# Attention probabilities scaled by the inverse mass on GpSimd ahead of the value products, with a new order on all engines

## What is computed

```python
x = x + attn_ref(layernorm(x), ...)              # RWKV: time mixing with a scan over tokens, then channel mixing
x = x + xattn_ref(layernorm(x), ctx, ctx)        # attention between the 16 heads of each token
x = x + ffn_ref(layernorm(x), U1, V1, b1, U2, V2, b2)   # low-rank feed-forward with gelu
```

```python
scores = einsum('bsqd,bskd->bsqk', qh, kh) / sqrt(16)     # 16 x 16 per token
scores = where(tril, scores, -1e18)
attn   = softmax(scores, axis=-1)
out    = einsum('bsqk,bskd->bsqd', attn, vh)
```

## Time and profile before

| | us |
|---|---|
| median of 3 runs | 1115.2 (1113.61 to 1116.03) |
| the profiled execution | 1110.05 |
| its span from first to last instruction | 1108.1 |

### The profile page before, as it was taken

One profiled execution on the slowest core, in us unless ns is written; L12 is line 12 of the kernel. 1 busy time (PEld: TensorE's weight loads), 2 busy tenths in 40 slices (PEclk: granted clock), 3 DMA queues, 4 the chain that ended last, 5 costly groups with the idle time before them and its releaser, 6 DMA issues.

```text
span 1108.1 us, 15665 instructions
## 1 busy us (share of the span) xinstructions
PE 977.9 (88%) x4160; PEld 613.5 (55%) x4160; DVE 956.1 (86%) x2185; ACT 863.3 (78%) x1585; POOL 903.4 (82%) x862
## 2 busy tenths in 40 slices
PE   4689698999999999999999999999999999889505
PEld 2347274756556474756556574757566574646303
DVE  5846899999999999999999999999999899777561
ACT  4876769799797979798897979798897969573603
POOL 0223989989898989989898989899898989898880
PEclk9799799999999999999999999999999999999756
DMA  7110020111110111111111011111111011111001
GB/s 235 38 38 1 0 58 1 20 58 20 58 19 18 41 20 57 19 57 20 57 19 33 25 19 57 19 57 20 57 21 38 1 20 39 20 39 20 20 0 39
DMA packets 38317, 38.72 MB, mean 35 GB/s; under 512 B 2660, under 2 KB 37864, under 8 KB 38248
## 3 DMA queue, kind: packets, MB, share of 16 engines
q1 hardware_dynamic: 29800, 29.58, 8.4%
q0 software_dynamic: 8448, 8.39, 5.2%
HBM read 29.58 MB, written 8.39 MB: 34 GB/s over the span
## 4 chain that ended last, share of the span: by engine, by line
ACT 25%; POOL 24%; DVE 21%; issue 17%; PE 8%; DVEq 0%; POOLq 0%; ACTq 0%
POOL prod L351 18%; DVE psum L1646 7%; ACT n L484 5%; ACT hidden L619 4%; PE psum L895 4%; POOL prod L329 3%; DVE stat L1420 3%; ACT v_dh L588 2%; ACT xr L509 2%; DVE psum L1587 2%; DVE x L1595 2%; ACT rr L546 1%; ACT xk L509 1%; ACT e L542 1%; PE psum L949 1%
## 5 line engine op out<-in xcount | busy, mean ns | idle before, releaser
L329 POOL TENSOR_TENSOR prod<-q,kv_ctx 128x256 f32<-128x256 f32 (+5 forms) x448 | 360.2, 859 | 65.9 <-ACT q L484 65.9
L351 POOL TENSOR_TENSOR prod<-prob,v_dh 128x256 f32<-128x256 f32 (+3 forms) x256 | 384.4, 1703 | 12.8 <-ACT prob L594 12.8
L895 PE MATMUL psum<-xk,w_key 128*128 128x512 f32 x512 | 230.7, 604 | 14.1 <-DVE xk L1483 14.1
L1646 DVE TENSOR_REDUCE psum<-prod 128x64 f32<-128x256 f32 (+3 forms) x256 | 192.2, 821 | 50.0 <-POOL prod L351 49.0
L949 PE MATMUL psum<-w_val,hidden 128*128 128x256 f32 x1024 | 226.3, 379 | 0.0
L949 PEld LDWEIGHTS psum<-w_val,hidden 128*128 128x128 f32 x1024 | 193.5, 190 | 32.5 <-issue 7.7
L1617 DVE TENSOR_REDUCE score<-prod 128x16 f32<-128x256 f32 (+5 forms) x448 | 176.0, 475 | 11.6 <-POOL prod L329 11.6
L895 PEld LDWEIGHTS psum<-xk,w_key 128*128 128x128 f32 x512 | 97.6, 193 | 131.4 <-issue 120.7
L444 ACT ACT_TABLE_LOAD x96 | 123.2, 1283 | 2.6 <-PEq L1805 0.9
L909 PE MATMUL psum<-ident,n 128*128 128x128 f32 x384 | 59.5, 288 | 68.2 <-ACT n L484 52.8
L909 PEld LDWEIGHTS psum<-ident,n 128*128 128x128 f32 x384 | 46.9, 148 | 98.2 <-issue 68.9
(11 more groups left out here) (97 smaller groups left out, 1782.9 us busy)
## 6 DMA issues: line engine op xcount, KB each, us to landing
x_in<-in_x SPq DMA_DIRECT2D x16, 512.0 KB, 5.3
kv_ctx<-in_ctx SPq DMA_DIRECT2D x16, 512.0 KB, 4.5
x<-in_x POOLq DMA_DIRECT2D x16, 512.0 KB, 5.8
out<-x SPq DMA_DIRECT2D x16, 512.0 KB, 3.3
w_key<-in_wkey SPq DMA_DIRECT2D x1, 1024.0 KB
w_val<-in_wval SPq DMA_DIRECT2D x1, 1024.0 KB
w_v<-in_v SPq DMA_DIRECT2D x2, 256.0 KB
w_k<-in_wk SPq DMA_DIRECT2D x1, 256.0 KB, 4.8
```

Of the source, the lines that this page charges most:

```text
L329: ins = pool.tensor_tensor(o, a, b, ALU.mult)
L351: ins = pool.tensor_tensor(o, ph[:, HB * n:HB * n + HB, 0:keys].unsqueeze(2).to_broadcast(shape), vh[:, :, 0:keys].unsqueeze(1).to_broadca ...
L895: mm = pe.matmul(to[:, :], w[:, fi, P * f:P * f + P], src[:, fi, :], start=(fi == 0), stop=(fi == CH - 1))
L1646: ins = dve.tensor_reduce(bank[SUM_BANK][:, row:row + HB * HD], src, AX.X, ALU.add)
```

## The change

- **Removed:** DVE's `over_mass`, two instructions a group on 512 columns in PSUM, and its semaphore `o_norm`. `third_residual` now waits for the sums alone.
- **Added:** POOL's `prob_by_mass`, two instructions a group on 512 elements in SBUF, in place on `prob`. It waits for `inverse_mass` of its half; `value_products` now waits for it. `sum_mass` of the next group waits for it too, since it overwrites `mass`.
- **Moved:** the order of the steps on PE, DVE, ACT and POOL, the numbers of PSUM banks, and the issue of a group's output DMA, now in the step after its feed-forward (`store_out(i - 5)` in place of `i - 4`).

```diff
+            def prob_by_mass(g, s):
+                rows = slice(2 * NH * s, 2 * NH * s + 2 * NH)
+                pool.wait_ge(inv_done, upto(g, 2, s + 1))
+                pool.tensor_tensor(prob[:, rows, :], prob[:, rows, :],
+                                   mass[:, rows].unsqueeze(2).to_broadcast([P, 2 * NH, NH]), ALU.mult)\
+                    .then_inc(prob_over_mass, 1)
...
-                pool.wait_ge(prob_done, upto(g, 2, t // 2 + 1))
+                pool.wait_ge(prob_over_mass, upto(g, 2, t // 2 + 1))
...
-            def over_mass(g, s):
-                rows = slice(2 * NH * s, 2 * NH * s + 2 * NH)
-                o = bank[SUM_BANK].rearrange("p (h d) -> p h d", d=HD)
+            def third_residual(g, par, s):
                 dve.wait_ge(v_sum, upto(g, 4, 2 * s + 2))
-                dve.wait_ge(inv_done, upto(g, 2, s + 1))
-                dve.tensor_tensor(o, o, mass[:, rows].unsqueeze(2).to_broadcast([P, 2 * NH, HD]), ALU.mult)\
-                    .then_inc(o_norm, 1)
...
-        KEY_BANK = [1, 6, 4, 3, 7, 0, 4, 6]
+        KEY_BANK = [7, 3, 3, 0, 4, 6, 4, 3]
```

More of the change, by code:

```diff
@@ L657, in step @@
                     relu(i - 3, 4)
+                    square(i - 3, 1)
+                if on(4):
+                    use_table(EXP_SET)
+                    probabilities(i - 4, 1)
+                if on(3):
+                    square(i - 3, 2)
+                if on(1):
+                    if on(3):
+                        act.wait_ge(rec_mm, upto(i - 3, 2))
+                    elif on(2):
+                        act.wait_ge(r_mm, upto(i - 2, 2))
+                    att_before_r(i - 1, 0)
+                if on(3):
+                    square(i - 3, 3)
+                    square(i - 3, 4)
                 if on(3):
@@ L713, in step @@
                     use_table(EXP_SET)
-                    ln_den(i - 2, 1)
+                    inverse_den(i - 2, 0)
                 if on(2):
                     use_table(EXP_SET)
-                    inverse_den(i - 2, 0)
-                if on(1):
-                    use_table(EXP_SET)
-                    back_ratio(i - 1, 1 - p)
-                if on(0):
-                    use_table(EXP_SET)
-                    both_ln(i)
+                    ln_den(i - 2, 1)
+                if on(3):
+                    values_by_dim(i - 3, 1 - p)
                 if on(2):
@@ L728, in step @@
                     use_table(EXP_SET)
-                    both_rstd(i)
+                    both_ln(i)
+                if on(1):
+                    split_rise(i - 1, 0)
                 if on(3):
@@ L742, in step @@
                     rstd_of(4, i - 4)
+                if on(1):
+                    use_table(EXP_SET)
+                    exp_e1(i - 1, 0)
+                    split_rise(i - 1, 1)
                 if on(4):
@@ L790, in step @@
                     normalise_2(i - 2, p)
+                if on(1):
+                    use_table(EXP_SET)
+                    exp_bonus(i - 1, 1)
+                if on(0):
+                    use_table(EXP_SET)
+                    back_ratio(i, p)
                 if on(4):
```

768 lines of the change are left out of this document (370 added, 398 removed).

## The result

| | before | after |
|---|---|---|
| median of 3 runs, us | 1115.2 | 1139.1 (1137.22 to 1139.21) |
| the profiled execution, us | 1110.05 | 1139.1 |
| its span, us | 1108.1 | 1137.4 |

The ratio is 1.0211, 95% interval 1.0187 to 1.0236: the changed kernel is 2.1% slower. Between the two profiled executions the span grew by 29.3 us; the prediction's sum for it was 29.1.

A forecast was written before the change was run, and what follows sets the result against it. A closed chain of POOL and ACT was taken to set the period: 56.3 + 7.5 = 63.8 us against 61.8. With +27.9, +0.4, +1.5 and -0.7, in all +29.1 on the 1115.2 median gave 1144 us, range 1131 to 1163.

The forecast's parts named there:

- the 14 periods: Steps from the first to the fifteenth group's score products: 63.8 us each against 61.8, +27.9 us in all.
- the closed chain through POOL and ACT: Loop from POOL's score products through `add_bb` and ACT's queries back to POOL, claimed to set the 61.84 us period.
- POOL's stretch A: From a group's first score products to its last `add_bb` on POOL: 54.57 us before, 56.3 predicted after.
- ACT's way round B: From the last `add_bb` through ACT to the next group's queries: 7.27 us before, 7.5 predicted after.
- What is removed: DVE's two multiplications, 1.4 us a step: costed at nothing in a repeating step, 0.7 us off behind the last value products.
- the chain has the same members and two instructions more: Reason given why the period grows from 61.8 to 63.8 us: POOL's work alone cannot be squeezed.
- The period from 968.52: Period to 1028.35, without `add_bb`: +2.3 us for multiplications and own wait, less the covered 1.93 us exponential wait, +0.4.
- The last group: Stretch from 1028.35 to 1076.95 us: +2.3 and -0.83, giving +1.5 us.
- The fill: Start of the program up to the first score products at 103.21 us: left unchanged, with 3 us either way.
- The tail: Stretch behind the last value products, where DVE's sums lose a multiplication: -0.7 us.
- Faster by the balance of engines: Rival for the repeating step: PE with little idle time sets it at 60.4 us, total 1097 us; chance 9%.
- The mass becomes the last: Rival at `prob_by_mass` 0: inverse mass comes a further 1.2 us late, period 65.0, total 1161 us; chance 15%.

The follow-up runs named there:

- removal alone: The kernel before without `over_mass`, the division by the mass left out, otherwise in the old order; 1111.98 us, ratio 0.9989.
- Without the division: The kernel after without `prob_by_mass`, so the same order with two POOL instructions a group fewer; 1128.65 us, ratio 1.0134 to the kernel before.
- second product on POOL: The kernel after with another POOL product of the same size ahead of each `prob_by_mass`, into a tile nobody reads; 1178.46 us, ratio 1.0583.

## Why the prediction was right, and where it wasn't

**The number.** The sum for the profiled execution was 1139.2 us; it took 1139.1. That these agree to 0.1 us is luck: the 14 periods were put 3.0 us too high (+27.9 predicted, 890.17 - 865.31 = +24.9 measured), the period behind them 1.9 and the stretch behind the last value products 1.4 too low, and these cancel. On the median 1144 was forecast and 1139.1 measured, inside the range. The 5 us between come from the level to which the sum was added: the profiled execution of before lay 5.1 us under its median, that of after on it.

**What bounds the kernel.** In the order of after the closed chain through POOL and ACT is there and closes as the prediction put it: from 229.86 to 293.26 us the chain of waits takes in all of POOL's stretch A and ACT's way round B. In the order of before it is not what set the step, and here "POOL's timeline shows one" fails: A held 0.76 us of waiting for the exponential and B 1.76 us for `mean_3` in every step, and a chain that waits for something off it has that much room. The chain traced there came to the exponential from the fourth norm. The page had a sign of it: of the chain that ended last, 18% lay on POOL's value products and 3% on its score products. The sum didn't suffer by this, since it built the new A and B from their members and left both waits out.

Nor is one chain alone. "What sets the step must be a closed chain" was taken as one; the runs show two close together in both orders: 61.85 and, with the first one shortened, 61.5 us in the old, 63.4 and 63.2 in the new. The 1.76 us for `mean_3` was a hint of the other. The prediction saw it and asked only what would fill it.

**What is removed.** Costed at nothing in a repeating step: right (removal alone, 0.9989). The reason was not the one given. `over_mass` lies on the chain of before (0.59 us at 594.60); what its removal frees, DVE spends waiting, for ACT's inverse deviation and for POOL.

**A.** 56.3 us predicted, 56.31 measured in the step shown; in the step from 804.09, at a granted clock of 1.00, it was 55.99. The multiplication takes 1.07 us (1.08 by the row of `shift_scores`), its own wait is 0.17 (0.1 taken, bounds 0 and 0.23), the wait for the mass about 0 (0.2 taken, a tie forecast).

**B.** 7.5 predicted, 7.45 measured, with the members named and `mean_3` covered; in three of the steady steps ACT still waited for it, 0.64 us in the period that ends at 548.97, which took 64.43.

**The cause of the 2 us.** Here the step "the chain has the same members and two instructions more" fails. As an account of POOL's chain it is right; as the reason why a period is 1.8 us longer it is not, since without the two instructions it is still 63.2. The sum had costed the new order only where it enters B. By the ratios the order brings 1.3% of the 2.1%, and the multiplications the rest, which in the profiles lies at the end more than in the steady steps: 2.75 us in 13 periods, 7.3 in the last two and the last group. In the old order, on the other hand, the same two instructions cost 6.9 us a period, most of it POOL's wait for the inverse mass. The right size came of two chains of nearly one length, of which the prediction computed the one that was 0.2 us longer.

**The period from 968.52.** +0.4 predicted, 62.14 - 59.83 = +2.3 measured. "the 1.93 us wait for the exponential is now covered by score products" fails: with no `add_aa` left POOL reaches the first `prob_by_mass` early and waits 2.09 us there for DVE's inverse (1018.76 above). Without the division this period took 59.55.

**The last group.** +1.5 predicted; 50.12 against 48.59 us. **The fill.** 0 predicted; -0.1. **The tail.** -0.7 predicted; 31.86 against 31.15 us, +0.7. The 0.7 us of DVE are there: from its last sums of values to PE's first transposes of the fourth norm it takes 1113.59 - 1105.57 = 8.02 us instead of 1085.73 - 1076.98 = 8.75, and 8.02 in the removal alone. What the prediction put at nothing is the feed-forward behind it, from these transposes to the last residual on DVE: 19.19 us instead of 17.77. PE does its products there in another order, and its clock rose from 0.50 to 1.00 some 10.7 us after the first transposes instead of 9.6. In the removal alone, with the old order, it rose after 11.3 us, and the stretch took 18.30.

**The rivals.** *Faster by the balance of engines* falls: DVE's relief is worth nothing, and room on POOL is not used (+2.1 us cost 2.1 and more). The rule of the Trainium skill (Perfetto Trace Analysis, Identifying the Most-Contended Engine), by which the engine with the highest occupancy is optimized first and TensorE's busy share doesn't count for that, points at DVE here. In this case it didn't pay: relieving DVE, busy 59.4 of 61.9 us, made no difference that can be measured, and shortening the waits through ACT to POOL, the least busy of the three, gave 1.1%. *The mass becomes the last* didn't happen in the steady steps (a tie to 0.1 us); it did at the end, and in the old order it would have cost three times what the rival priced.

## What to carry to other kernels

A chain that repeats with the step is not yet the one that sets it: where it holds a wait for something off it, as here for the exponential, follow that wait. When a repeating step is tied to a closed chain, look for the second one before costing an edit: shorten the first on paper and follow which wait comes last then, since what an edit gives is bounded by the difference of the two, while what it adds to the longer one is paid in full. A change that comes with a new order is two changes; running the order without the added work separates them. And a wait at which an instruction stands idle for a microsecond or two (here for `mean_3`) is often the place where the second chain crosses the first.

## What the runs showed of the hardware that was not expected

**A short wait of PE inside a busy step was followed by a lower clock.** In the kernel after PE waited 1.47 us for the second residual (PE's timeline), and the granted clock (1.00 is the level of 2.4 GHz, 0.50 that of 1.2) fell to 0.57 and 0.86 in the two windows behind it and was back at 1.00 in the next:

```profile
544.83 1.13 PE L1013 MATMUL psum<-b_row,ones 1*128 1x512 f32 x4 [1.47 <-DVE x L1602]
...
546.95 5.41 PE L912 MATMUL psum<-w_o,num 128*128 128x256 f32 x16
```

```profile
544.00:547.00 3.00, 2.17 (x13) 1.07 (x13) 2.89 (x13) 2.14 (x8) 1.27 (x1) 1.00 0.00 0
547.00:550.00 3.00, 3.00 (x10) 2.46 (x9) 3.00 (x12) 2.97 (x8) 1.03 (x2) 0.57 0.00 0
550.00:553.00 3.00, 3.00 (x11) 2.19 (x10) 2.86 (x10) 3.00 (x7) 3.00 (x4) 0.86 0.02 7
```

The 16 output projections took 5.41 us instead of 3.72. After a wait of 0.66 us at the same place one step later it stayed at 1.00. The length of the wait alone doesn't decide it: in the kernel before, PE waited 1.41 us in every steady step for ACT's copy of the fourth norm (L976) and once 1.91 us, and the clock stayed at 1.00; in the kernel after without the division a wait of 1.46 us for the second residual (414.20) left it at 1.00, one of 1.48 (541.50) didn't. With the second product on POOL PE waits longer there in every step (44.8 us in 14), and this kernel's two lengths of period go with the stretch at the lower clock behind the wait. The 16 output projections ahead of the period of 65.5 us (697.01 to 762.53) took 4.30 us, those ahead of that of 67.3 (762.53 to 829.83) 5.27. A window in each:

```profile
696.00:699.00 3.00, 3.00 (x12) 2.59 (x13) 2.75 (x12) 2.97 (x8) 1.99 (x3) 0.82 0.00 0
761.00:764.00 3.00, 3.00 (x10) 1.95 (x9) 2.72 (x11) 2.97 (x8) 1.47 (x2) 0.50 0.00 0
```

The waits ahead of them were alike, 2.58 and 2.67 us; in the second case the engine was still at the level of 1.2 GHz at 761 to 764 us, and POOL waited 0.53 and 1.11 us for DVE in the period that followed. So in this run the longer chain on POOL came with a slower PE, and the step grew by more than the time that was added. That the wait is what lowers the clock is not shown.

**The end of the program can take 5 us longer at a lower clock.** In the profiled execution of the removal alone (1114.05 us) the period from 966.82 took 65.37 us, against 59.83 in that of before. PE, granted clock and all as above, had little to do from 960 on and stayed between the two levels; in the same stretch of the kernel before (961.7 to 991.7 us) it had 0.83, 0.88 and 0.95. POOL's first value products then waited 5.66 us for the exponential, against 1.93:

```profile
960.00:970.00 10.00, 6.18 (x15) 3.13 (x13) 5.66 (x21) 6.71 (x15) 6.07 (x6) 0.68 0.01 2
970.00:980.00 10.00, 7.07 (x34) 4.69 (x33) 6.32 (x19) 1.99 (x6) 10.00 (x15) 0.81 0.19 54
980.00:990.00 10.00, 7.49 (x40) 5.22 (x40) 4.40 (x13) 8.85 (x16) 9.10 (x12) 0.70 0.16 53
```

The ten runs of this kernel lie at 1108.7 to 1109.9 and at 1111.7 to 1114.3 us. Whether this stretch parts them, and the profiled execution of before from its median, wasn't seen in a second profile.

**A DVE product with both operands in SBUF is slow beside POOL.** In the run with the multiplication on DVE (group with shape and count, busy, mean ns; then two instances on DVE's timeline):

```profile
L1638 DVE TENSOR_TENSOR prob<-prob,mass 128x512 f32<-128x512 f32 x32 | 43.0, 1345 | 1.1
```

```profile
319.39 0.74 DVE L1638 TENSOR_TENSOR prob<-prob,mass 128x512 f32<-128x512 f32 x1
...
331.96 1.75 DVE L1638 TENSOR_TENSOR prob<-prob,mass 128x512 f32<-128x512 f32 x1
```

At 319.39 POOL was waiting for this very product; at 331.96 it was in the value products, and the same 512 elements took 1.75 us. The 32 instances go from 0.69 us with POOL idle to 2.80. The removed `over_mass`, whose sums lay in PSUM, took 0.70, and there POOL was busy all through it. The Trainium skill (SBUF — State Buffer, Who interferes with whom) states that a VectorE instruction with two SBUF inputs contends with a GpSimd instruction that reads SBUF; these rows agree.
